# Own result buffers for the last quads, results copied ahead of row numbers, and stores in pairs of blocks: a Mamba block with a mixture of experts on one core

## What is computed

```
x1  = layernorm(x + (mamba(x) + x))
top 4 of 16 experts per token, weights cw           (router)
act = silu(x1 @ Wg[e].T) * (x1 @ Wu[e].T)           256 -> 128
y   = sum over the 4 experts of cw[e] * (act @ Wd[e].T)   128 -> 256
y   = y + silu(x1 @ Ws_g.T) * (x1 @ Ws_u.T) @ Ws_d.T      (shared expert)
out = layernorm(x1 + y)
```

## Time and profile before

| | |
|---|---|
| median of 3 runs | 616.09 us (615.06 to 617.58) |
| the profiled execution | 614.0 us |
| its span, first to last instruction | 612.2 us |
| TensorE busy | 536.0 us (88%) |
| VectorE busy | 445.5 us (73%) |
| ScalarE busy | 373.0 us (61%) |
| GpSimd busy | 327.0 us (53%) |
| mean granted TensorE clock | 0.965 of full speed |

### The profile page before, as it was taken

The page is one execution under the profiler, slowest core; times in us unless marked ns, Lnnn a source line. Parts: engine busy times, 40 slices in busy tenths (PEclk is TensorE's granted clock), DMA queues, the critical chain, the costliest instruction groups (busy, mean ns, idle before and its releaser), DMA issues.

```text
span 612.2 us, 11884 instructions
## 1 busy us (share of the span) xinstructions
PE 536.0 (88%) x3200; PEld 455.1 (74%) x3200; DVE 445.5 (73%) x1122; ACT 373.0 (61%) x952; POOL 327.0 (53%) x368
## 2 busy tenths in 40 slices
PE   2868999999989999889958989899999989998592
PEld 2546676677767777667647889799999989987582
DVE  3868899999998999998867467634444368787575
ACT  3674866846557565555543377677787767676352
POOL 2051302571855718537274747777777666667620
PEclk9988899899998999989979999999999999999797
DMA  8971402341232322312658356987666499873994
GB/s 207 293 249 47 152 35 105 118 157 60 98 119 75 146 73 99 126 39 98 215 187 314 127 191 183 315 272 241 214 195 211 127 371 309 299 257 119 386 298 141
DMA packets 70151, 111.22 MB, mean 182 GB/s; under 512 B 12644, under 2 KB 52965, under 8 KB 69704
## 3 DMA queue, kind: packets, MB, share of 16 engines
q1 hardware_dynamic: 52304, 71.11, 36.5%
q0 software_dynamic: 13056, 35.68, 15.9%
q10 hardware_dynamic: 4728, 3.67, 1.9%
HBM read 61.77 MB, written 50.74 MB: 184 GB/s over the span
## 4 chain that ended last, share of the span: by engine, by line
PE 59%; DVE 20%; issue 9%; ACT 6%; DMA 3%; POOL 1%; SPq 1%; ACTq 0%; POOLq 0%; DVEq 0%
PE psum L700 9%; PE psum L861 5%; PE psum L863 4%; PE psum L862 4%; PE psum L843 4%; PE psum L757 4%; PE psum L680 3%; PE psum L642 3%; DVE xc L1252 3%; PE psum L644 3%; PE psum L643 3%; PE psum L885 3%; PE psum L952 3%; PE psum L887 2%; PE psum L886 2%
## 5 line engine op out<-in xcount | busy, mean ns | idle before, releaser
L596 POOL DMA_INDIRECT x_buf<-row,row_id x128 | 125.0, 977 | 117.6 <-DVE row_id L1433 81.5
L634 POOL DMA_INDIRECT y_buf<-y_out,y_ids x104 | 105.8, 1017 | 52.3 <-issue 30.5
L1607 DVE TENSOR_TENSOR t_lo<-psum,t_hi 128x512 fp32r<-128x512 f32 x72 | 48.8, 686 | 52.6 <-ACT t_hi L1113 52.6
L861 PE MATMUL psum<-ew_gu_hi,t_hi 128*128 x288 | 84.8, 294 | 2.1 <-DVE t_lo L1607 1.0
L863 PE MATMUL psum<-ew_gu_hi,t_lo 128*128 x288 | 81.4, 283 | 0.0
L862 PE MATMUL psum<-ew_gu_lo,t_hi 128*128 x288 | 81.4, 283 | 0.0
L1252 DVE SCALAR_TENSOR_TENSOR xc<-psum,cw_taps,xc 128x511 f32<-128x511 f32 (+2 forms) x96 | 71.8, 747 | 8.3 <-ACT halo_x L976 5.9
L588 POOL TENSOR_TENSOR m<-xc,zs 128x512 f32<-128x512 f32 x32 | 42.5, 1355 | 64.7 <-DVE shift L1313 48.0
L700 PE MATMUL psum<-wout,m 128*128 128x256 f32 x256 | 61.3, 400 | 14.9 <-DVE m L1277 14.9
L700 PEld LDWEIGHTS psum<-wout,m 128*128 128x128 f32 x256 | 50.7, 201 | 25.4 <-DVE m L1277 18.1
L642 PE MATMUL psum<-x_hi,win_hi 128*128 128x512 f32 x128 | 56.1, 439 | 13.9 <-DVE win_lo L1572 10.8
(11 more groups left out here) (221 smaller groups left out, 1376.3 us busy)
## 6 DMA issues: line engine op xcount, KB each, us to landing
tiles_in<-x_buf SPq DMA_DIRECT2D x144, 144.0 KB
y_in<-y_buf SPq DMA_DIRECT2D x32, 512.0 KB, 7.8
xT<-in_x_T SPq DMA_DIRECT2D x8, 512.0 KB
xtok<-in_x_tok SPq DMA_DIRECT2D x8, 512.0 KB, 3.4
gu_hi_buf<-w_hi_now SPq DMA_DIRECT2D x8, 512.0 KB, 2.6
out_dram<-res ACTq DMA_DIRECT2D x7, 512.0 KB, 3.6
x_buf<-pad_row SPq DMA_DIRECT2D x17, 144.0 KB
raw_gu<-in_wg_T SPq DMA_DIRECT2D x16, 128.0 KB, 2.9
```

Source lines behind the costliest of these rows:

```text
L596: nc.gpsimd.indirect_dma_start(out=x_buf, out_offset=bass.IndirectOffsetOnAxis(ap=row_id[t % ROWS][:, b, k:k + 1], axis=0), in_=row[t % RO ...
L634: nc.gpsimd.indirect_dma_start(out=y_buf, out_offset=bass.IndirectOffsetOnAxis(ap=y_ids[:, q % IDS, i:i + 1], axis=0), in_=y_sent[:, i, :] ...
L861: pe.matmul(o, t_hi[par][:, k, r], w_hi, start=k == 0, stop=False)
L1607: V.tensor_tensor(t_lo[par][:, k, :], x_turned(q, k), f32(t_hi[par][:, k, :]), ALU.subtract) \
```

## The change

1. `y_out` gets two more buffers, which lie in slots 0 and 1 of `tiles_in`; quads 34 and 35 use these, and `out_free` waits for nothing there. The row counts that SyncE waits for take in their two new semaphores.
2. On ScalarE result(q-2) comes ahead of result_rows(q+1).
3. On TensorE the waits of down(q-1), for `a_l` and `y_evac`, and the load of its expert numbers stand ahead of turn_x(q+2, 1). In the last iteration turn_act(35) stands ahead of these waits and of down(34).
4. On VectorE act_low(35) stands ahead of the last block_sum, not behind it.
5. ScalarE issues the stores of blocks 8 to 19 in a row behind the normalization of block 19; blocks 24 to 27 are stored in two pairs. SyncE stores blocks 28 to 31 in two pairs, each once VectorE has done it.

```diff
@@ -192,6 +192,7 @@
         y_out += y_in[0:2]
+        y_out += [tiles_in[:, b, :, 0:D] for b in range(2)]
         ew_d_hi = p2sb("ew_d_hi", [P, E, D], F32R)
@@ -293,9 +294,14 @@
         ACT_NORMED = SUB * (2 * HG - 1)
+        STORED_AT = {3: ((0, 4),), 7: ((4, 8),), 19: ((8, 12), (12, 16), (16, 20)), 23: ((20, 24),),
+                     25: ((24, 26),), 27: ((26, 28),)}
+        STORES = sum(map(len, STORED_AT.values())) + 2
 
...
 
+            if u >= NQ - 2:
+                return RING + u - (NQ - 2)
             return u % RING if half_of(j, u) == 0 else u % 2
@@ -310,12 +316,16 @@
 
+            if u >= NQ - 2:
+                return
             y_left(eng, j, u - (RING if half_of(j, u) == 0 or half_of(j, u - 2) == 0 else 2))
...
             for b in range((RING, 2)[h]):
-                at_least(eng, f"y_sent{b}_{h}", 16 * SUB * (end // RING if h == 0 else (end - HQ) // 2))
+                at_least(eng, f"y_sent{b}_{h}", 16 * SUB * (end // RING if h == 0 else (min(end, NQ - 2) - HQ) // 2))
+            for q in range(NQ - 2, end):
+                at_least(eng, f"y_sent{out_slot(0, q)}_{h}", 16 * SUB)
 
@@ -525,11 +535,12 @@
             load_late(LAST_BLOCKS)
-            g = 2 * HG - 1
-            at_least(sp_, "o_done_dve", SUB)
-            sp_.dma_start(out.rearrange("(n p) d -> p n d", p=P)[:, SUB * g:SUB * (g + 1), :],
-                          res[:, SUB * g:SUB * (g + 1), :]).then_inc(s["stored"], 16)
-            at_least(sp_, "stored", 16 * HALVES * HG)
+            for i in range(0, SUB, 2):
+                b = ACT_NORMED + i
+                at_least(sp_, "o_done_dve", i + 2)
+                sp_.dma_start(out.rearrange("(n p) d -> p n d", p=P)[:, b:b + 2, :],
+                              res[:, b:b + 2, :]).then_inc(s["stored"], 16)
+            at_least(sp_, "stored", 16 * STORES)
 
@@ -907,12 +918,18 @@
                         table_mm(1)
+                    experts = tile_experts(q - 1)
+                    if q + 1 == NQ:
+                        turn_act(j, u)
+                    at_least(pe, "a_l", q)
+                    at_least(pe, "y_evac", q - 1)
                     if q + 2 < NQ:
                         turn_x(j, u + 2, range(1, KD))
-                    down(j, u - 1, tile_experts(q - 1))
+                    down(j, u - 1, experts)
                     if q == LATE_TABLE:
                         at_least(pe, "table_done", 4)
-                    turn_act(j, u)
+                    if q + 1 < NQ:
+                        turn_act(j, u)
                 if q == 0:
@@ -1145,6 +1162,12 @@
 
+            def store(first, end):
+
+                at_least(act, "o_done", end)
+                act.dma_start(out.rearrange("(n p) d -> p n d", p=P)[:, first:end, :],
+                              res[:, first:end, :]).then_inc(s["stored"], 16)
+
             def out_norm(k):
@@ -1153,10 +1176,8 @@
                       scale=o_rstd[k % 2][:, b - first:b - first + 1]).then_inc(s["o_done"], 1)
-                    if i == SUB - 1:
-                        at_least(act, "o_done", b + 1)
-                        act.dma_start(out.rearrange("(n p) d -> p n d", p=P)[:, b + 1 - SUB:b + 1, :],
-                                      res[:, b + 1 - SUB:b + 1, :]).then_inc(s["stored"], 16)
+                    for a, z in STORED_AT.get(b, ()):
+                        store(a, z)
 
@@ -1183,12 +1204,12 @@
                         x_high(j, u + 2, 0)
+                    if q > DEEP:
+                        result(j, u - 2)
                     if q == DEEP:
...
                         result_rows(j, u + 1)
-                    if q > DEEP:
-                        result(j, u - 2)
                     if q + 1 < NQ:
@@ -1689,6 +1710,8 @@
                         act_low(j, u - 1)
+                    if q + 1 == NQ:
+                        act_low(j, u)
                     if q + 2 < NQ:
@@ -1716,7 +1739,6 @@
 
-            act_low(0, NQ - 1)
             norm(0)
```

More of the change, by code:

```diff
@@ L220, in mamba_moe @@
             tile_in0 tile_in1 tile_in2 tile_in3 t_mm t_h t_l gu_mm g_silu e_mul at_mm a_h a_l y_mm
-            y_evac y_id_done y_sent0_0 y_sent1_0 y_sent2_0 y_sent3_0 y_sent0_1 y_sent1_1
+            y_evac y_id_done y_sent0_0 y_sent1_0 y_sent2_0 y_sent3_0 y_sent0_1 y_sent1_1 y_sent4_1 y_sent5_1
             y_in0 y_in1 y_in2 y_in3 y_in4 y_in5 y_in6 y_in7 y_in8 y_in9 y_in10 y_in11 y_in12 y_in13 y_in14 y_in15
```

## The result

The changed kernel took **611.98 us** in the median of 11 runs (609.1 to 615.43), the kernel before, run beside it, 615.88 us (612.61 to 618.15): ratio 0.9943, 95% interval 0.9922 to 0.9963. It is faster by 3.9 us where 9.6 were forecast (616.1 to 606.5), and lies 0.5 us above the range of 604.0 to 611.5. The profiled executions give the same difference: 610.12 us with a span of 608.4 against 614.0 and 612.2.

The account below looks back on a forecast made before the run. TensorE's late down(35) was taken to bound the end, unless loads are late; loop -2.2, quads 34 and 35 -6.4, stores -1.0 sum to -9.6 us: 614.0 to 604.4 profiled, 606.5 median, range 604.0 to 611.5.

Parts of the forecast that it names:

- Loop, -2.2 us: Loop, ScalarE and TensorE: result ends sooner, so the wait before down vanishes in 18 iterations; -2.2 us, bounds 0 and -3.9.
- Quads 34 and 35, -6.4 us: Tail, TensorE and ScalarE: result(34) no longer waits, down(35) starts at 570.7, block 18 at about 576.6; -6.4 us.
- The gap of 2.5 us that is left: TensorE between down(34) and down(35): the remaining idle time was expected to leave the clock at full pace.
- that rival: Down(35) and direct blocks: the clock falls all the same, 8.2 in place of 5.8 us; 608.9 us, chance 0.05.
- VectorE, no cost: VectorE's tail: act_low(35) before the last block_sum; first pair done at 576.5, just when TensorE asks for it.
- Loads, nothing: Last loads: GpSimd ends at 583.5, the last load lands between 592.6 and 594.6; cost taken as nothing.
- the 594.9 of the sum: TensorE's forecast end, with the last load wanted 1.3 us earlier, at 593.6.
- the 1.7 of the upper bound: Last load landing at 594.6: TensorE would end at 596.6, 1.7 us later.
- the first rival: End of the kernel: the last loads bound it, with deferred stores in their way; 606.5 + 1.7 = 608.2 us, chance 0.22.
- Stores, -1.0 us: End of the kernel: storing the last blocks in pairs gives -1.0 us, bounds +0.4 and -1.6; deferred stores cost nothing.
- Slower by results that meet the scatter: Loop, quads 22 to 33: copies and transposes wait behind scatters, up to 13.3 us lost; 622.0 us, chance 0.04.
- The buffers do what they should: Denies the rival that GpSimd stays the limit and the last load arrives at 597.5; 613.3 us, chance 0.05.

Follow-up runs that it names:

- the second such profile: The changed kernel plus identity matmuls before turn_act(35) and down(35), stores of blocks 0 to 7 also deferred behind block 19: two runs, 730.88 us (0.9873) and 729.55 us (1.0039).
- SyncE shifted: The changed kernel with SyncE's loads of summed blocks and their wait two iterations later: two runs, 724.62 us (ratio 0.9878) and 729.58 us (0.9951).

## Why the prediction was wrong, point by point

- **Loop, -2.2 us: right in the loop, wrong at the end.** The waits vanished as reckoned and had brought 1.7 us by down(22). The step that failed is the sentence that the tiles, loaded three iterations ahead, cost nothing. It looked at the slots that ScalarE frees and not at the one place where SyncE's queue waits for GpSimd's sends. I had the 1.09 us wait for a tile in the trace of before and read it as small, not as the mark of a second pace setter. What arrived is -0.24 us. That GpSimd's backlog is a cause is read from the two traces, not tested, and it explains only some 0.5 us of the 1.0: its last send of half 0 came 1.17 us sooner, down(22) 1.72. From down(24) on nothing is added either: the 0.3 us won by down(26) go at the wait before the transposes at 521.78.
- **Quads 34 and 35, -6.4 us: mechanism right, the clock wrong.** Result(34) waits for nothing, turn_act(35) slipped into the gap, and at full clock block 18 is 10.03 us behind down(34) against the 9.93 of the sum. The step that failed is "The gap of 2.5 us that is left is about that before down(34), after which down ran at full pace". The gap before down(34) was not safe either: the clock fell in down(34), and 3.5 us at block 18 went with it. I priced that rival at 2.4 us, for down(35) and the direct blocks only, and gave it 0.05 on the strength of a single row. The Trainium skill (TensorE: Matmul & The Clock Gate, HAM oscillation) tells of a TensorE that waits for data between short bursts and starts each burst cold. The waits in its example are longer than the 1.54 and 0.17 us here, so I stretched it when I called this rival the likely one by that rule; what the runs show is a fall in eight of ten profiles and none in two, one of these with the same waits.
- **VectorE, no cost: right as far as block 18, but with nothing to spare at full clock.** The first pair starts at 576.65, where 575.8 was reckoned, and TensorE does not wait for it. At full clock the pair ended when block 18 could start (715.36 and 716.11), and in the second such profile TensorE waited 1.09 us for it. At the end the text left out that VectorE has eight statistics to do behind its last pair.
- **Loads, nothing: wrong, and enough by itself to hold the end.** The step that failed is "I take nothing". GpSimd ended at 582.93 (583.5 in the text). I had the last load issued 2.5 us behind it, as before, and landed by 594.6 at the latest; it was issued at 588.4, 5.4 us behind, because the scatter needed 4.1 us from the send's end to SyncE's first issue where it had needed 1.2, and it was in at 595.9. With its pair of 0.7 us and the block of 1.3 us, TensorE could not end before 597.9, which is 3.0 us behind the 594.9 of the sum, not 0 and not the 1.7 of the upper bound. So the first rival's mechanism came true, at a higher price. The clock hid it on TensorE, which took up block 31 0.6 us after its pair was ready, but the chain that ended last runs over the loads. The two shortfalls do not add: either one alone takes nearly all of the 3 us that the tail lacks.
- **Stores, -1.0 us: right**, -0.93 from the last LayerNorm's first copy to the end. The deferred stores were not free: the third's issue held ScalarE for 1.1 us, at a time when it had idle time.
- **The rivals.** Slower by results that meet the scatter did not happen: in the loop ScalarE never waits for `y_sent`. The buffers do what they should.

The sum that the profile gives along TensorE: 614.0 - 0.24 - 2.82 - 0.73 = 610.2, against 610.12 us. The forecast's 604.4 for the same execution is missed by 5.7 us: some 2.0 in the loop, 3.6 by the clock and the last loads together, 0.3 at the end, with rounding.

## What to carry to other kernels

When a change closes one of two gaps of TensorE and leaves the other, price the rest of the stretch at the low clock too, unless many executions show it at full; a single row after a gap is no proof. Before a long TensorE stretch is called the limit of the end, follow the chain that ended last: here two paths, the slow clock and the last loads, ended within 0.25 us of each other, and mending only one of them would by these rows have gained 0.25 us at most, an estimate. A wait removed upstream lengthens the queue at the slowest helper: before counting the gain, look for the next place at which any queue waits for that helper (here GpSimd's sends, on which SyncE's tile loads hang). And if work is moved earlier, look at what large DMAs it now runs into: the last scatter of 128 KB had landed 1.2 us after the end of its send where no 512 KB store had been issued in the 2.4 us before (but for one at the very end), and 2.3 to 3.2 us after it with a 512 KB store issued 1.0 to 1.5 us before that end.

## What the runs showed of the hardware that I had not expected

- The clock's fall is not a function of the last gap alone. The waits ahead of down(34) were the same 1.54 and 0.17 us in two profiles of the change, and the clock fell a little later in the second (0.70 and 0.85 in its window); in one profile with SyncE shifted it did not fall until later, with the same waits. The kernel before idled more in the window ahead (0.33 of 2 us busy against 0.46) and kept its clock in the profile shown.
- 16 identity matmuls of 128 columns did not delay down(35) (0.24 us behind result(34)) and the clock was 1.00 in the stretch from 704 to 714 us of that profile. Where the clock had already fallen, after an idle time of 4.06 us, the last ten of them cost 0.45 us.
- On five chips ScalarE's instructions waited on a queue outside the trace for up to 20 us at a time; such waits are 4 to 14% of the chain that ended last, and everything took 18 to 22% longer, at unchanged busy times of VectorE, ScalarE and GpSimd. What queue that is stays open.
